# Gather passes of a graph network: tile numbers taken from packed words by division and remainder instead of shift and mask

## What is computed

```python
# layer 1: attention over the edges, 8 heads of 32 values (self loops are handled apart)
e = leaky_relu(a_src[src] + a_dst[dst], 0.2)
e = exp(e - m[dst])
denom = segment_sum(e, dst)
out = segment_sum(xh[src] * (e / denom[dst]), dst)

# layer 3: one of two message networks per edge type, summed into the destination
msgs = where(rel == r, edge_nn(feat[src], W_rel[r], b_rel[r]), msgs)
agg = segment_sum(msgs, dst)
gates = agg @ W_ih.T + b_ih + b_hh      # then an LSTM-like cell and three small layers
```

## Time and profile before

| what | us |
|---|---|
| median of three runs | 7916.3 (7910.52 to 7924.33) |
| span of the profiled execution, first to last instruction | 7482.7 |
| median of the runs less that span | 433.6 |
| attention pass, first to last gather issue | 3469.2 to 4595.3 |
| message pass, first to last gather issue | 6357.1 to 7427.1 |

### The profile page before, as it was taken

How to read it: one execution, slowest core, us unless ns; L and a number is a source line. 1 busy time by engine, 2 the same in 40 slices (tenths; PEclk the granted TensorE clock), 3 DMA queues, 4 the chain that set the end, 5 groups by cost and what they waited for, 6 DMA issues and landing times.

```text
span 7482.7 us, 126299 instructions
## 1 busy us (share of the span) xinstructions
PE 6524.4 (87%) x29550; PEld 4866.3 (65%) x29551; DVE 3687.6 (49%) x10588; ACT 2350.1 (31%) x6423; POOL 3090.6 (41%) x3455
## 2 busy tenths in 40 slices
PE   5888888999999999998888987599999997777777
PEld 2333333788877878776666666477778886666666
DVE  9999999111111112224777777612223333555554
ACT  6888887000000001112222221312223333222222
POOL 5777776000100011114777775200011111777775
PEclk9999999999999999998877777799999998899898
DMA  5555557877987797775333333688897775444443
GB/s 194 211 215 211 214 213 250 316 273 274 336 292 272 280 339 260 253 255 173 101 99 99 99 99 103 234 324 290 294 357 245 249 246 188 119 122 121 121 123 95
DMA packets 668862, 1601.14 MB, mean 214 GB/s; under 512 B 77659, under 2 KB 306989, under 8 KB 668605
## 3 DMA queue, kind: packets, MB, share of 16 engines
q1 hardware_dynamic: 543133, 1232.09, 46.5%
q0 software_dynamic: 125488, 365.75, 16.1%
HBM read 1208.17 MB, written 390.27 MB: 214 GB/s over the span
## 4 chain that ended last, share of the span: by engine, by line
PE 51%; POOL 11%; issue 7%; DMA 7%; DVE 4%; ACT 1%; DVEq 1%; SPq 0%; POOLq 0%; ACTq 0%
PE psum L1343 35%; POOL ring L1096 6%; PE psum L1192 4%; PE psum L1619 3%; POOL tbuf L1096 3%; PE psum L1591 2%; DMA g_own<-own_dram 2%; POOL rb L1096 2%; DMA slab<-adj 2%; PE psum L1603 1%; PE psum L1522 1%; PE psum L1187 1%; PE psum L1292 1%; PE psum L1301 1%; DMA tbuf<-rel_table,idx_slot 1%
## 5 line engine op out<-in xcount | busy, mean ns | idle before, releaser
L1343 PE MATMUL psum<-X,slab 128*128 128x512 f32 x12495 | 3104.2, 402 | 87.8 <-DMA slab<-adj 43.7
L1343 PEld LDWEIGHTS psum<-X,slab 128*128 128x128 f32 x12495 | 2345.2, 190 | 618.7 <-DVE g_x L2336 89.3
L2486 DVE TENSOR_TENSOR acc<-acc,psum 128x264 f32 (+1 forms) x1660 | 704.2, 424 | 508.1 <-PE psum L1619 369.1
L1008 POOL DMA_DIRECT2D table<-s_tab x147 | 80.2, 545 | 1905.2 <-DVE s_tab L2083 1905.2
L974 POOL TENSOR_SCALAR hot_j<-iota_j,col_now 128x392 bf16<-128x392 bf16 x587 | 783.3, 1346 | 0.0
L1464 PE MATMUL psum<-hot_j,hot_key 128*128 128x392 bf16 x2348 | 583.6, 330 | 190.5 <-DVE hot_j L2299 149.0
L2313 DVE SCALAR_TENSOR_TENSOR staged<-staged,keep_all,psum 128x392 fp32r<-128x392 f32 x1174 | 717.0, 611 | 7.6 <-PE psum L1464 5.2
L1706 ACT ACTIVATE key_sq<-iota_row,edge_key 128x128 f32<-128x128 f32 x2055 | 657.4, 389 | 2.3 <-DVE staged L2288 2.3
L2083 DVE TENSOR_TENSOR s_tab<-psum,s_tab 128x256 fp32r<-128x256 f32 x196 | 82.7, 422 | 1141.5 <-ACT s_tab L1663 1141.5
L2299 DVE TENSOR_SCALAR hot_j<-iota_j,edge_col 128x392 bf16<-128x392 bf16 x1761 | 567.3, 349 | 0.0
L1658 ACT COPY s_hT<-psum 128x256 f32<-128x256 f32 x273 | 101.7, 373 | 1349.2 <-PE psum L1187 1349.2
(11 more groups left out here) (417 smaller groups left out, 8822.3 us busy)
## 6 DMA issues: line engine op xcount, KB each, us to landing
slab<-adj SPq DMA_DIRECT2D x385, 1344.0 KB, 6.5
slab<-adj SPq DMA_DIRECT2D x315, 896.0 KB, 5.9
adj<-staged SPq DMA_DIRECT2D x1174, 196.0 KB, 1.9
X<-table SPq DMA_DIRECT2D x33, 1792.0 KB, 13.0
table<-s_tab POOLq DMA_DIRECT2D x147, 256.0 KB, 3.1
g_own<-own_dram POOLq DMA_DIRECT2D x35, 896.0 KB, 8.4
own_dram<-s_out POOLq DMA_DIRECT2D x147, 128.0 KB, 5.5
acc<-zero_rows SPq DMA_DIRECT2D x2, 6600.0 KB, 27.4
```

Source lines behind the costliest of these rows:

```text
L1343: last = nc.tensor.matmul(sums_of(j), slab[:, slab_at(c), u, j * P:(j + 1) * P], X[:, x_at(p, d), :], start=(d == 0), stop=(d == KT - 1))
L2486: V.tensor_tensor(a, a, psum[:, bank, 0:w], ALU.add).then_inc(sem("summed"), 1)
```

## The change

```diff
         def tiles_of_word(word):
 
-            return [((word >> TILE_BITS * v) & ((1 << TILE_BITS) - 1)).with_bounds(min_val=0, max_val=T - 1) for v in range(HALF)]
+            return [(word // (1 << TILE_BITS * v) % (1 << TILE_BITS)).with_bounds(min_val=0, max_val=T - 1) for v in range(HALF)]
```

## The result

The changed kernel took 7895.93 us (median of 10 runs, 7886.04 to 7911.37), the kernel before on the same occasion 7913.3 us (10 runs, 7910.48 to 7929.15). The medians are 17 us apart. The ratio of the runs is 0.9973, 95% interval 0.9964 to 0.9982, so 0.27% faster, or 21 us by that ratio. Forecast were 7915 us in a range of 7896 to 7932, and no difference that can be measured.

The account below looks back on a forecast made before the run. The prediction took POOL's gather issue to bound both gather passes. Worth 0 in each pass and 1.5 us off outside the gathers' cover turned 7916.3 into 7914.8, forecast 7915 us, range 7896 to 7932.

Parts of the forecast that it names:

- closed row: Both gather passes: POOL issues gathers back to back, 0.30 us gap after each, and no other engine holds it up.
- an add starts 0.13 us earlier after its matmul: Message pass, VectorE: the shorter chain starts adds earlier, but POOL does not wait for them; worth 0.
- TensorE's part: Attention pass logits: nine register instructions a half go, 0.65 us, 0.2 given back; POOL does not wait for it, worth 0.
- VectorE's part of the attention pass: At most 0.04 us a step comes off, all becoming longer waits for gathered rows; worth 0.
- The fused instruction: VectorE's address computation before each add: grows from 57 ns to 90 ns, bounds 57 and 192, stated sign 70 to 120.
- The row of five operations: Trace row of another fused instruction (minimum, multiplications, additions), 85 ns, taken as nearest match for the new one's price.
- the 129 ns from add to add: VectorE, one add's end to the next one's start: forecast to shorten from 290 to 161 ns.
- The period of two adds in the attention pass: VectorE's add, scaling, next add: 0.72 us, forecast to become 0.68 to 0.72.
- Slow division: Rival, attention pass: a fused instruction above 0.41 us makes VectorE the limit; at 0.5 us 75 us slower, 7990; chance 0.08.
- fewer collisions: Rival, message pass: earlier one-hot builds overlap gathers less, 11 us faster, up to 22; 7904, ends 7893 to 7912; chance 0.12.
- More collisions: Rival, message pass: builds moved ahead of gather starts stretch them, 20 us less 10 from others; 7925, up to 7935; chance 0.08.
- the prediction's example: Attention pass gather at 7417.40: stretched 0.59 us by a one-hot build overlapping it 0.72 us, four fifths of the rule's size.

Follow-up runs that it names:

- e0: The kernel before, unedited, measured and profiled once more where updates are late: 7996.3 us, ratio 0.9998.
- e4: The whole change against the kernel before, on an occasion without late updates: 7488.07 against 7483.31 us, ratio 1.0004.
- e17: The whole change once more against the kernel before, on an occasion without late updates: ratio 0.9999.
- e1: Division and remainder on VectorE alone, in both passes, against the kernel before, where updates are late: ratio 0.9976.
- e3: Division and remainder in the message pass alone, against the kernel before, where updates are late: ratio 0.9963.
- e11: The whole change once more against the kernel before, where updates are late: ratio 0.9952.
- e8: The kernel before with two more masks (register instructions) a step in the message pass, where updates are late: ratio 1.0073.
- e2: Division and remainder on TensorE alone, in the attention pass, against the kernel before, where updates are late: ratio 0.9987.
- e12: Division and remainder in the attention pass alone, on both engines, against the kernel before, where updates are late: ratio 0.9996.
- e7: Two shifts in place of division and remainder, both passes, against the kernel before, without late updates: ratio 1.002.
- e6: The kernel before with two more register instructions a step in the message pass, without late updates: ratio 0.9993.
- e10: The kernel before with one more unused matmul ahead of each in the message pass, where updates are late: ratio 1.0064.
- e14: The kernel before with the message pass's matmuls on 128 of 256 columns, where updates are late: ratio 0.9981.

## Why the prediction was wrong, and where it was right

**The step that failed** is the first one, that POOL stands in a closed row: "So no other engine holds POOL up, and a pass takes as long as its 830 gathers take to issue." It was read rightly from the trace, and the trace wasn't of the runs to be predicted. The sign was there, and the prediction explained it away: "the median of the runs shown is 433.6 us above that span and does not change by it". Start and end of a launch take 1.9 us. The other 432 had to be somewhere inside the span, 5.8% of it, and by e0 nearly all of such a difference is in the gather passes, where the change is: 1352.2 + 1333.2 against 1127.2 + 1071.0 us, 487 of the 513 us between the two spans. In the profile of the result POOL waits some 223 and 214 us for indices beyond its gap in the two passes, where the prediction had none.

**What the slack was worth.** "In the message pass an add starts 0.13 us earlier after its matmul ... Worth: 0" holds where updates are in time (e4 1.0004, e17 0.9999). Where they are late, the message pass is 27 us shorter (1333.2 to 1305.8; e1 and e3, with the same code there, 1308.4 and 1306.6). That is the term that was put at nothing. For the occasion of the result itself there is no profile of the kernel before, so that its 17 us arise in the same way is inferred from the other three. Its gain of 0.27% (0.18 to 0.36) is smaller than the 0.48% (0.35 to 0.62) of e11, with a kernel before of 7913.3 against 8000.6 us; why is open. What the runs support for the way of it: POOL's indices wait for a matmul, the matmul for a bank that an add frees, the add for the adds queued before it; this loop has slack as long as updates come in time, and none behind a late bunch. POOL's waits in four versions fall in the order of the chain's length. That each microsecond goes through the queued adds is not shown; e8 lost more than they hold, and e11 gained more.

**TensorE's part**, "Worth: 0", gave 10 us there (e2 0.9987). **VectorE's part of the attention pass**, also 0, cost something. With e1 and e3 it is +10 us, with e2 and e12 +7, alone +21, and in the whole change (-38 by e11, with -30 and -10 for the other two) about 2. Each figure but the third is a difference of such ratios, so they don't contradict each other; the medians give 10, 13, 14 and 10. A loss of 10 to 20 us is what the runs support, and its cause stays open.

**The fused instruction was mis-sized.** Expected 90 ns, measured 158, inside the bounds of 57 and 192 and outside the stated 70 to 120. With two shifts in place of division and remainder it is 116: so division and remainder cost some 42 ns more than two shifts. The row of five operations, 85 ns, was no match, and division is not all of the reason: with two shifts there are five operations without a division, and they take 31 ns more than that row. Of the 129 ns from add to add, 57 came: 293 to 236 ns. The estimate of 81 ns for a register instruction with its gap was somewhat high as well: two of them make 138 ns in e8, 69 each. The period of two adds in the attention pass fell from 0.72 to 0.68, as forecast (e17):

```profile
4004.93 0.42 DVE L2486 TENSOR_TENSOR acc<-acc,psum 128x264 f32 x1
...
4005.27 0.41 DVE L2506 TENSOR_TENSOR tbuf<-tbuf 128x256 f32<-128x256 f32 x1
4005.61 0.42 DVE L2486 TENSOR_TENSOR acc<-acc,psum 128x264 f32 x1
```

Slow division, at 0.41 us, did not come: the longest of these fused instructions takes 189 ns.

**Collisions.** The result of 7895.93 us lies among the times that the prediction gave to "fewer collisions" (7893 to 7912), but that is luck: where updates are late, the message pass's gathers got longer with the change, not shorter (mean 973 ns in e0, 998 in e11). "More collisions" was right in its mechanism on an occasion without late updates, but not for this change: there two builds moved and nearly cancelled (31 us of stretch to 34). One more step of the same direction, two shifts, lengthens the pass by 20.6 us, where the prediction had 20 us, less 10 from other builds. The Trainium skill's rule (SBUF — State Buffer, "Who interferes with whom"), that the later of the two blocks fully, would stretch the gather of e7 by the overlap, 7003.39 - 7002.63 = 0.76 us; the row shows 1.58 - 0.95 = 0.63, four fifths of it, as in the prediction's example.

**Right, then:** no measurable difference from the shorter chain wherever POOL's row is closed (e4, e17), nor from a longer one (e6). **Wrong:** that it is closed in the runs that count.

## What to carry to other kernels

Hold the span of a profile against the time of the runs that you predict before you read anything else in it. Here the two are 1.9 us apart when they belong together; where they lie much further apart, the profile is of other conditions, and slack read from it is no slack. A chain that is hidden in the steady state can be paid after each disturbance, as here, so shortening it may gain where an undisturbed profile shows no wait; price it by what a disturbed run shows. Count waits by their place in the loop, not only in total: that is what told queued adds from a second wait in e8. And judge a change of a few parts in a thousand on both kinds of occasion: here two shifts are the equal of the best where updates are late (0.9953) and 0.2% slower where they are not.

## What of the hardware was not expected

- **Two kinds of occasion**, 6.9% apart for the same kernel (7483.3 and 7998.4 us). On one of them TensorE's semaphore updates come late in bunches, in the gather passes only, with waits of up to 9.8 us behind them; from 3600 to 4500 us, in the attention pass, there are 50 to 56 bunches in each of the twelve profiles, and none in the eight of the other kind. In the message pass POOL is held up at the same two places of the loop in every one of the twelve, 79 to 81 times in 83 turns. The same twelve have 271 to 377 update records too few for the 2514 matmuls that make one in the gather passes, the other eight at most 3. Neither more nor less work for TensorE (e10, e14) removes the bunches. The cause is open; that they keep step with the program's loop speaks against something that strikes at random.
- **Register operations.** One by itself takes 45 ns on VectorE and 36 on TensorE's queue. Fused, two shifts add 59 and 47 ns to the address computation (57 to 116, 46 to 93), division and remainder 101 and 81 (to 158 and 127). With the division, 147 ns of instructions on VectorE became 158: all that is gained are the gaps between instructions, and two instructions fewer shorten the add-to-add chain by 57 ns all the same.
- **A faster VectorE can slow POOL.** A build 0.06 us ahead of a gather costs 0.63 us, and the places repeat with the loop, so that a fused instruction 42 ns shorter (158 to 116) moved one build in four to the worst place in nearly every loop.
